# Moving a matrix product of the edge updates ahead of a scatter-add

## The reference, cut to what matters

```python
# edges e, nodes n; B = 128, F = 32; x is the input of the layer (after a layer norm)
s, v   = hs[src], hv[src]                    # (e, F) and (e, F, 3), from x @ w_in2f
msg_s  = concat(t_s1 * a1, t_s2 * a5)        # (e, 2F) scalars
msg_v  = ...                                 # (e, 2F, 3) vectors
sum_s, sum_v = segment_sum(msg_s), segment_sum(msg_v)      # by node: 8F = 256 numbers a row
o_s = sum_s @ w_f2o1_s / sqrt(2F)            # (n, 128)
o_v = sum_v @ w_f2o1_v / sqrt(2F)            # (n, 128, 3)
o_s = (softplus(o_s) - log 2) @ w_f2o2_s / sqrt(B)
o_v = o_v @ w_f2o2_v / sqrt(B)               # nothing nonlinear between the two products
y   = x + concat(o_s, o_v)                   # then layer norm: the rows x3
```

## Time and profile before

| | |
|---|---|
| median of 3 runs | 2283.05 us (2282.64 to 2285.45) |
| the profiled execution | 2283.68 us |
| its span, first to last instruction | 2282.0 us |
| PE busy | 1894.0 us (83%) |
| DVE busy | 1505.0 us (66%) |
| ACT busy | 1161.8 us (51%) |
| POOL busy | 938.4 us (41%) |
| moved to and from HBM | 316.65 MB, mean 139 GB/s |

### The profile page before, as it was taken

The page is one execution under the profiler, slowest core; times in us unless marked ns, Lnnn a source line. Parts: engine busy times, 40 slices in busy tenths (PEclk is TensorE's granted clock), DMA queues, the critical chain, the costliest instruction groups (busy, mean ns, idle before and its releaser), DMA issues. The chain is left out here.

```text
span 2282.0 us, 25087 instructions
## 1 busy us (share of the span) xinstructions
PE 1894.0 (83%) x5922; PEld 970.1 (43%) x5922; DVE 1505.0 (66%) x2634; ACT 1161.8 (51%) x2333; POOL 938.4 (41%) x1048
## 2 busy tenths in 40 slices
PE   5999998599999999999999948624435999999930
PEld 2444443244444444444444425313323555555510
DVE  5365553277777777777777648177637877777867
ACT  2344443255555555555555412245537777777744
POOL 3212112266666666666666655445531111111026
PEclk9999999799999999999999968855556999999975
DMA  7742112444444444444444365533327443443444
GB/s 256 243 167 62 19 14 37 143 146 150 159 158 156 154 154 150 150 150 150 154 158 156 126 226 110 90 105 79 81 50 269 167 151 133 155 151 128 147 148 148
DMA packets 146225, 316.65 MB, mean 139 GB/s; under 512 B 18817, under 2 KB 32034, under 8 KB 145638
## 3 DMA queue, kind: packets, MB, share of 16 engines
q1 hardware_dynamic: 114646, 235.45, 29.4%
q0 software_dynamic: 28160, 75.82, 13.2%
q10 hardware_dynamic: 3344, 4.51, 0.7%
HBM read 176.64 MB, written 139.79 MB: 139 GB/s over the span
## 5 line engine op out<-in xcount | busy, mean ns | idle before, releaser
L667 PE MATMUL d_p_h<-w3a,d_xT 128*128 128x512 f32 x632 | 287.1, 597 | 25.1 <-DMA d_xT<-in_xT 25.1
L667 PE MATMUL d_p_o<-d_w,d_uT 128*128 128x512 f32 x632 | 286.2, 596 | 3.0 <-ACT d_uT L742 3.0
L667 PE MATMUL d_p_p<-d_wr,d_x1T 128*128 128x512 f32 x632 | 288.4, 600 | 0.0
L552 POOL TENSOR_SCALAR d_small<-d_mv 128x1 f32<-128x1 f32 x158 | 80.8, 512 | 299.6 <-DVE d_mv L793 151.6
L824 DVE TENSOR_TENSOR d_zz<-d_yg,d_xbeta 128x512 f32<-128x512 f32 x79 | 136.9, 1733 | 97.7 <-POOL d_yg L875 97.7
L667 PEld LDWEIGHTS d_p_h<-w3a,d_xT 128*128 128x128 f32 x632 | 121.1, 192 | 178.5 <-issue 178.5
L667 PEld LDWEIGHTS d_p_o<-d_w,d_uT 128*128 128x128 f32 x632 | 120.3, 191 | 154.9 <-issue 150.3
L735 ACT ACTIVATE d_yn<-d_y,d_small 128x512 f32<-128x512 f32 x79 | 64.3, 813 | 228.5 <-POOL d_small L557 228.5
L667 PEld LDWEIGHTS d_p_p<-d_wr,d_x1T 128*128 128x128 f32 x632 | 115.6, 193 | 116.6 <-issue 116.6
L763 ACT ACTIVATE d_x<-d_zz,d_small 128x512 f32<-128x512 f32 x79 | 64.2, 813 | 175.3 <-POOL d_small L557 175.3
L284 PE MATMUL m_p_H<-m_xT,m_w 128*128 128x512 f32 x320 | 147.3, 615 | 4.8 <-ACT m_xT L325 4.8
(11 more groups left out here) (275 smaller groups left out, 4345.1 us busy)
## 6 DMA issues: line engine op xcount, KB each, us to landing
state<-d_empty SPq DMA_DIRECT2D x80, 264.0 KB, 2.1
sum<-m_tile_sum SPq DMA_DIRECT2D x10, 2048.0 KB
pair_rows<-p_rows SPq DMA_DIRECT2D x40, 512.0 KB
pair_x<-x SPq DMA_DIRECT2D x40, 512.0 KB
out_rows<-pair_rows SPq DMA_DIRECT2D x40, 512.0 KB
d_xT<-in_xT SPq DMA_DIRECT2D x79, 256.0 KB
d_z<-sum SPq DMA_DIRECT2D x79, 256.0 KB
d_x<-in_x SPq DMA_DIRECT2D x79, 256.0 KB
```

The source lines that it names most:

```text
L552: nc.gpsimd.tensor_scalar(tmp, var, factor, add, ALU.mult, ALU.add).then_inc(done, 1)
L667: last = nc.tensor.matmul(out[:, :], lhsT[:, c, :], w[:, c, :], start=(c == 0), stop=(c == KB - 1))
```

## The change

The two products o1 (scalars) and o1 followed by o2 (vectors) are linear, so they can be made on the tile sums before these are added to the table. The table then holds 512 numbers a row (`update`) instead of 256 (`sum2`), and the loop keeps the nonlinearity and the second product of the scalars.

- `dense_phase`: `fill` writes `update` (256 KB a tile) instead of `sum2` (128 KB).
- `edge_rows_phase`: at the start o1v@o2v is made once (DVE waits for the load of o1v and o2v ahead of `norm(0)`; PE and ACT do a transpose, a product and three copies; POOL clears three half tiles). `tile_sums` becomes two products with 128 columns, so that the sums come out transposed; `tile_update` (four products with 128 columns) and `update_out` (ACT, 512 wide) are new. DVE takes `message(t-2)` in round t instead of `message(t-1)`, and the orders of PE, ACT and POOL change.
- `values_phase`: gone are `turn_sums`, `first`, the identity product and three of the four products of `second`, and on ACT `sums_turned_out`, `first_product_out` and `second_product_out`. New are `turn_ssp` (two transposes), `ssp_turned_out` and `x3_squares` (two squares); DVE's `moments` become `residual`, which stands behind `pair_leaky`; POOL gathers rows of 512 into four buffers and does so behind the work on the state.

```diff
 def dense_phase
-                sp.dma_start(rows(k.sum2, i), empty[:, 0:8 * F]).then_inc(tables_set, 16)
+                sp.dma_start(rows(k.update, i), empty[:, 0:D]).then_inc(tables_set, 16)
 def edge_rows_phase
 sync
+            for half in range(2):
+                sp.dma_start(o1v[half * 2 * F:(half + 1) * 2 * F, :], k.L2_o1v).then_inc(o1v_in, 16)
+            sp.dma_start(o2v[:, :], k.L2_o2v).then_inc(o1v_in, 16)
+            sp.dma_start(w_s[0:2 * F, :], k.L2_o1s).then_inc(w_in, 16)
 gpsimd
-                pool.wait_ge(s_out, t + 1)
+                pool.wait_ge(u_out, t + 1)
-                pool.indirect_dma_start(k.sum2[:, :], at_rows(k.unique[:, 0, t:t + 1]), tile_sum[t % 2][:, :], None,
+                pool.indirect_dma_start(k.update[:, :], at_rows(k.unique[:, 0, t:t + 1]), update[t % 4][:, :], None,
-            for t in range(T + 2):
+            for t in range(T + 4):
+                if t >= 4:
+                    scatter(t - 4)
                 if t + 2 < T:
                     gather(2 * t + 5)
                     gather(2 * t + 4)
-                if 0 <= t - 2 < T:
-                    scatter(t - 2)
 vector
+            dve.wait_ge(o1v_in, 48)
+            nc.vector.tensor_scalar(o2v[:, :], o2v[:, :], float(B) ** -0.5, None, ALU.mult).then_inc(o2_scaled, 1)
-            for t in range(T + 1):
+            for t in range(T + 2):
                 if t < T:
                     norm(t)
-                if t:
-                    message(t - 1)
+                if t >= 2:
+                    message(t - 2)
 scalar
+            def update_out(t):
+                act.wait_ge(u_done, t + 1)
+                if t >= 4:
+                    act.wait_ge(scattered, 16 * (t - 3))
+                nc.scalar.activation(update[t % 4][:, :], p_U[t % 2][:, :], ACT.Copy).then_inc(u_out, 1)
-            for t in range(T + 1):
+            for t in range(T + 3):
                 if t < T:
                     x2_rows(t)
+                if 2 <= t < T + 2:
+                    sum_out(t - 2)
+                if t < T:
                     turn_out(t)
-                if t:
-                    sum_out(t - 1)
+                if t >= 3:
+                    update_out(t - 3)
 tensor
-                nc.tensor.matmul(p_S[t % 2][:, 0:8 * F], k.same_src[:, t, :], edge[t % 2][:, :], start=True, stop=True
-                                 ).then_inc(s_done, 1)
+                for half in range(2):
+                    last = nc.tensor.matmul(p_S[t % 2][:, half * P:(half + 1) * P],
+                                            edge[t % 2][:, half * P:(half + 1) * P], k.same_src[:, t, :],
+                                            start=True, stop=True)
+            def tile_update(t):
+                pe.wait_ge(s_out, t + 1)
+                if t >= 2:
+                    pe.wait_ge(u_out, t - 1)
+                vector = p_U[t % 2][:, B:D].rearrange("p (b c) -> p c b", c=3)
+                for c in range(4):
+                    last = nc.tensor.matmul(p_U[t % 2][:, 0:B] if c == 0 else vector[:, c - 1, :],
+                                            sumT[t % 2][:, (c // 2) * P:(c // 2 + 1) * P],
+                                            (w_s, w_high, w_low, w_high)[c][:, :], start=True, stop=True)
-            for u in range(T + 1):
+            for u in range(T + 2):
+                if u >= 2:
+                    tile_sums(u - 2)
                 if u < T:
                     turn(u)
+                if u >= 2:
+                    tile_update(u - 2)
+                if u < T:
                     features(u)
-                if u:
-                    tile_sums(u - 1)
 def values_phase
 gpsimd
-            for u in range(AHEAD):
-                gather_sums(u)
+            gather_rows(0)
+            gather_rows(1)
             for step in range(STEPS):
-                for u in (2 * step + AHEAD, 2 * step + AHEAD + 1):
-                    if u < 2 * T:
-                        gather_sums(u)
                 t = step - 4
                 if 0 <= t < T:
                     scatter_state(t)
                     if t + 1 < T:
                         gather_state(t + 1)
+                if step + 2 < T:
+                    gather_rows(step + 2)
 tensor, order of a step (a = step, b = step - 1, ...)
-   second(b,0) turn_x3(c,0) turn_x3(c,1) second(b,1) turn_sums(a,0) turn_scores(d) queries(c) spread_scores(d)
-   first(a,0) turn_sums(a,1) values(d) first(a,1) keys(c) tile_sums(d)
+   turn_x3(c,0) turn_x3(c,1) turn_ssp(b) queries(c) turn_scores(d) second(b) spread_scores(d)
+   values(d) keys(c) tile_sums(d)
 scalar, order of a step
+   away_from(d) x3_turned_out(c,0) x3_turned_out(c,1) state_factors(e) ssp_turned_out(b) first tile
+   query_out(c) scores_out(d) second tile logarithms(a) weights(d) x3_squares(b,0) x3_squares(b,1)
+   x3_rows(b) third tile
 vector, order of a step
-   scores(d) new_maximum(e) moments(b,0) merge(e) pair_leaky moments(b,1) tile_maximum(d) ...
+   scores(d) new_maximum(e) merge(e) pair_leaky residual(b) tile_maximum(d) ...
+            def residual(t):
+                b, rows = t % 2, y[t % ROWS_AHEAD]
+                dve.wait_ge(second_done, t + 1)
+                nc.vector.tensor_copy(rows[:, :, 0:B], p_R[:, 0:2 * B].rearrange("p (s b) -> p s b", s=2)
+                                      ).then_inc(second_out, 1)
+                dve.wait_ge(second_out, t + 1)
+                for s in range(2):
+                    nc.vector.scalar_tensor_tensor(out=rows[:, s, :], in0=rows[:, s, :], scalar=1.0, in1=rows_of(t, s),
+                                                   op0=ALU.mult, op1=ALU.add, accum_out=total[b][:, s:s + 1]
+                                                   ).then_inc(y_done, 1)
+                ...
+                nc.vector.tensor_scalar(neg[b][:, :], total[b][:, :], -1.0 / D, None, ALU.mult).then_inc(ready, 1)
```

More of the change, by code:

```diff
@@ L1274, in edge_rows_phase @@
         scratch = [sb(f"scratch{i}", [P, D]) for i in range(2)]
-        edge, part, tile_sum = ([sb(f"{n}{i}", [P, w]) for i in range(2)]
-                                for n, w in (("edge", 8 * F), ("part", 3 * F), ("tile_sum", 8 * F)))
-        p_T, p_F, p_S = ([ps(f"p_{n}{i}", [P, D]) for i in range(2)] for n in "TFS")
+        edge, part, sumT = ([sb(f"{n}{i}", [P, w]) for i in range(2)]
+                            for n, w in (("edge", 8 * F), ("part", 3 * F), ("sumT", 2 * P)))
+        update = [sb(f"update{i}", [P, D]) for i in range(4)]
+        o1v, o1vT, o2v = sb("o1v", [P, B]), sb("o1vT", [B, P]), sb("o2v", [B, B])
+        w_s, w_low, w_high = (sb(n, [P, B]) for n in ("w_s", "w_low", "w_high"))
+        p_T, p_F, p_S, p_U = ([ps(f"p_{n}{i}", [P, D]) for i in range(2)] for n in "TFSU")
         w_in = sem("w_in")
@@ L1524, in state_parts @@
             return buf[:, 0:ATT].rearrange("p (h f) -> p h f", h=HEADS)
-        def turn_number(step, place):
-            before = 0
-            for i in range(step):
-                before += 2 * (0 <= i - 2 < T) + 2 * (i < T)
-            if place >= 2:
-                return before + 2 * (0 <= step - 2 < T) + place - 2
-            return before + place
         block = ctx.enter_context(nc.Block())
@@ L1628, in second, with turn_ssp @@
-            def second(t, s):
-                u = 2 * t + s
-                pe.wait_ge(ssp_done, t + 1)
-                if u:
-                    pe.wait_ge(y_done, u)
-                else:
-                    pe.wait_ge(w2_scaled, 2)
-                nc.tensor.matmul(p_R[:, :], k.ident[:, :], rows_of(t, s), start=True, stop=False)
-                vector = p_R[:, B:D].rearrange("p (d c) -> p c d", c=3)
-                for c in range(4):
-                    last = nc.tensor.matmul(p_R[:, 0:B] if c == 0 else vector[:, c - 1, :],
-                                            outT[t % 2][:, s, c * P:(c + 1) * P],
-                                            (w2s if c == 0 else w2v)[:, :], start=False, stop=(c == 3))
+            def turn_ssp(t):
+                pe.wait_ge(ssp_done, t + 1)
+                if t:
+                    pe.wait_ge(ssp_out, t)
+                for s in range(2):
+                    last = nc.tensor.transpose(p_O[:, s * P:(s + 1) * P], ssp[t % 2][:, s, :], k.ident[:, :])
+                last.then_inc(ssp_turned, 1)
@@ L1641, in second @@
+            def second(t):
+                pe.wait_ge(ssp_out, t + 1)
+                if t:
+                    pe.wait_ge(second_out, t)
+                else:
+                    pe.wait_ge(w2_scaled, 1)
+                for s in range(2):
+                    last = nc.tensor.matmul(p_R[:, s * B:(s + 1) * B], sspT[t % 2][:, s, :], w2s[:, :],
+                                            start=True, stop=True)
                 last.then_inc(second_done, 1)
@@ L1834, in _ @@
                 if a < T:
-                    first_product_out(a, 0)
-                    sums_turned_out(a, 1)
+                    logarithms(a)
```

(7 more changed lines are left out.)

204 lines of the change are left out of this document (90 added, 114 removed).

## The result

The changed kernel takes 2216.49 us (median of 4 runs, 2215.89 to 2218.52), the kernel before 2283.57 in runs beside it: ratio 0.9707, 95% interval 0.969 to 0.9724. The forecast was 2201 within 2178 to 2230, so the time lies in the range, 15 us above the point. The profiled execution of after took 2215.89 us with a span of 2214.2, 67.8 less than before.

A forecast was written before the change was run, and what follows sets the result against it. PE was taken to bound the dense stage and steady loop, a circle of ACT and PE queues the edge rows; savings of 37 (edge rows), 37 (steady loop) and 8 (first steps) from 2283.7 gave 2201 us, range 2178 to 2230.

The forecast's parts named there:

- Dense stage and fill: Dense stage: 128 KB more a tile is covered by PE and costs 0, upper end 5 us.
- Edge rows, the round: Edge rows: opening the circle of queues cuts a round from 8.53 to 6.3 us, bound by DVE; 36 us saved.
- Edge rows, the end: End of edge rows: one more product, copy and scatter hang behind, but scatters no longer queue; no change.
- The start: Start of edge rows: DVE's wait for the o1v and o2v load ahead of `norm(0)` costs 1 to 2 us.
- First steps: Loop's first five steps: ACT loses copies and no longer waits within `second`; 8 us saved, between 0 and 14.
- Steady loop: Steps 5 to 20: rounds of 18.5 us after one pair, 20.1 after two; 288.7 against 325.5, 37 us saved.
- The last three steps and the closing stage stay: End of the loop and closing stage: no change in time, 0 us.
- PE at 75 to 80% of the steady loop: Sign of being right: PE busy about 75 to 80% of the steady loop.
- The rule of the Trainium skill: Bursts of products separated by waits start at a halved clock; taken to agree for edge rows, only in part for loop.
- The sum: Whole kernel: 37 + 37 + 8 = 82 us saved from 2283.7, giving 2201.7.
- the likeliest case: Whole kernel: all three savings arrive, reaching from 2187 to 2215 us; chance 0.60.
- the clock rival: Steady loop: clock falls ahead of `spread_scores` delay one-pair rounds 1.5 us, 12 us in all; 2213 to 2228; chance 0.18.

The follow-up runs named there:

- edges_alone: The kernel before with only the edge rows' new order (message, copy and tile sums lag two tiles); ratio 0.9814.
- load_back: The changed kernel with 14 idle 128x512 products a step, 12.0 us, put on TensorE ahead of queries and values; ratio 1.0366.
- warm: The changed kernel with 4 idle products, 3.4 us, ahead of each step's queries on TensorE; ratio 0.9776.
- warm_two: The changed kernel with 2 idle products, 1.7 us, ahead of each step's queries on TensorE; ratio 0.968.
- loop_alone: The changed kernel with the old order (lag of one tile) in the edge rows; ratio 0.9937.
- squares_warm: The changed kernel with x3 squares ahead of weights on ScalarE and 2 idle products ahead of spread scores in steps with two-pair entries; ratio 0.9694.
- squares_warm_next: The changed kernel with squares ahead of weights, update copied sooner, and 2 idle products ahead of spread scores in steps after two-pair entries; ratio 0.9616.
- update_sooner: The changed kernel with the copy of a tile's update placed behind the squares of the next edge rows; ratio 0.9693.

## Why the prediction was right, point by point

- *Dense stage and fill: right.* 128 KB more a tile made it no longer; 150 became 162 GB/s. The 3.3 us by which after comes sooner to the edge rows are a difference between executions and were no part of the forecast: in one set of runs edges_alone, with the narrow `fill`, gets there at 1499.5 us, load_back and warm, with the wide one, at 1499.6 and 1499.4.
- *Edge rows, the round: right.* 6.17 us where 6.3 was forecast, and between 1530 and 1636 the trace has no wait of DVE; it is VectorE's own sum. PE was mis-sized: 109.5 us for 20 tiles are 5.5 each, and up to 1643 it is busy for 78% of the stretch, where 6.1 to 6.35 and "over 85%" stood.
- *Edge rows, the end: the step that failed.* "The scatters no longer queue; I take no change." They don't queue in the rounds, where one comes every 6.17 us, but they do after the last, where tiles become ready faster than the 5.65 us that one scatter-add of 512 takes. The term was +6.6 us (33.6 against 27.0). The start, up to the end of the first `norm`, cost 2.8 us (11.4 against 8.6) where 1 to 2 was taken: DVE begins `norm(0)` only behind the load of o1v and o2v, for which it waits 7.10 us, most of it within the stage; before, it waited 3.20 us there for the first gather. The rounds gave 39.8 where 39 was counted. So -30.4 instead of -37.
- *First steps: right*, -8.2.
- *Steady loop: right in its mechanism and nearly in its size.* 18.5 and 20.1 us as worked out from ACT's chain and DVE's sum, the wait at `merge` of 3.0 us in the mean of the eight one-pair steps where "3.4" and "about 3" stood (3.6 to 3.9 in four of them; 2.6 or less in the other four, where DVE has first waited 1.2 to 2.1 us for `keys`, which the sum had not seen). The forecast of 288.7 is nearly what warm_two has (289.4), whose `queries` all keep the upper clock; the change has 292.3.
- *The clock: a rival that came true in part.* I gave 0.18 to falls ahead of the scores that cost 12 us or more. In the steady steps they cost 2.9 us (read from warm_two). In steps 20 to 22 the lines of the last steps show them directly: `queries` take 5.40 us where before's took 3.66, so that DVE waits 1.49 us for the scores and the first step is 1.6 us longer (in loop_alone, with `queries` of 3.70 us there, it is as long as before); then `values` take 6.58 us where before's took 3.70, and the second step is 3.3 us longer. These are the 4.9 us.
- *"The last three steps and the closing stage stay": wrong by 7.3 us.* The 4.9 are the slow products just named. The other 2.4 hold DVE's wait of 1.88 us for the last `values`, and that is only in part the clock. These `values` were slow before as well (5.40 us, now 6.57), and their scores now come 1.2 us later (5.7 us ahead of the end of `tile_maximum`, before 6.9), because ACT copies them behind a pair's tile. How much of the 7.3 belongs to the change is uncertain by about 2 us, as the same loop differs between executions: steps 20 to 22 took 31.9 us before and 33.6 in edges_alone, which has the old loop (clock 0.95 and 0.85), and 36.7 in after and 34.2 in loop_alone, which has the new one (0.80 and 0.86).
- *PE at 75 to 80% of the steady loop: wrong.* It is 87%, because slow products count as busy: at full clock 15.3 us a step (load_back) against 17.0 busy.
- *The rule of the Trainium skill* (TensorE: Matmul & The Clock Gate, "HAM oscillation — how this bites in real kernels"), that bursts separated by waits start slow: here the burst behind a wait of 2.36 us in squares_warm does so (3.33 for 2.05 us, 5.71 for 3.70), as do the six `queries` of after behind 2.24 or 2.25 us, and the burst behind a wait of 1.8 us at 1952.15 in after does not (3.70). The trace agrees with it in part: in nine of 15 steps the `queries` do not pay, and `values` are slow at times with no such wait ahead of them. That goes with the low chance I gave it.
- *The sum: in the range, with some luck.* The profiled execution is 14.2 us above the 2201.7 of the sum: 6.6 in the edge rows, 3.8 in the steady loop and 7.3 behind it, less 0.2 in the first steps and the 3.3 us of the dense stage that nothing in the forecast earned. 2216 is 1 us outside the reach that I gave to the likeliest case (2187 to 2215) and inside that of the clock rival (2213 to 2228), though that rival's 12 us in the steady loop were 2.9.

## What to carry to other kernels

Do one half of a change at a time: here the reordering that came along with it gave 42 us in the edge rows, while the products moved there cost 9, and paid only through the 6 us a step that they took off TensorE in the loop. When an engine is no longer the bound, look at its waits for what the clock does behind them before shortening another engine's queue: moving two squares shortened the steady loop by 4 us, and with two idle products that held the clock up in the right steps by 17 us, 0.8% of the kernel. And a chain of dependent transfers that hides in a loop's rounds shows at its end, where nothing spaces them.

## What the runs showed of the hardware

- A plain f32 product of 128x512 is two rows in the trace, 0.86 us together at 2.4 GHz (12.0 us for the 14 of load_back) and about 1.6 at mostly 1.2 (6.58 for four); counting rows as products was an error by a factor of 2.
- After a wait of 2.36 us on TensorE the next products ran partly at 1.2 GHz; with two idle products in it 0.64 us of the wait were left, and the whole loop kept its pace. In a step where PE waited 0.28 us at most the clock also fell (5.40 us for `values` at 1984.98 in squares_warm_next), which I can't explain from these traces.
- The same scatter-add of 512-wide rows has its issue on POOL in 1.56 us in the tail and mostly in 2.0 to 2.2 in the rounds of update_sooner, against 1.6 to 1.75 in those of the change; the rounds stayed 6.16 us, so it was hidden, and its cause stays open.
